# Decoder layer on one core: denominator sums by two merged DMA chains, projection in f16 parts

## The reference

```python
q = heads(x @ Wq)                      # x is layer-normed; 16 heads of 32
k_s, v_s = x @ Wkv_short;  k_l, v_l = x @ Wkv_long
bias = -abs(pos[None, :] - pos[:, None]) * (1 - decay_factor)
out = alpha * attention(q, k_s, v_s, bias) + (1 - alpha) * attention(q, k_l, v_l, None)
x = x + out @ Wo
x = x + cross_attention(ctx, layernorm(x), mask)
x = x + fp4_linear(silu(gate(x)) * up(x), w_down)    # gate, up: fp4_linear too
```

## Time and profile before

| | before |
|---|---|
| median of 3 runs | 5346.45 us |
| profiled execution | 5346.38 us |
| its span | 5344.6 us |
| busy over the span: PE, DVE, ACT, POOL | 96%, 77%, 54%, 50% |
| mean granted TensorE clock | 0.986 |
| moved by DMAs that POOL issues (q0) | 469.79 MB |

### The profile page before, as it was taken

The page is one execution under the profiler, slowest core; times in us unless marked ns, Lnnn a source line. Parts: engine busy times, 40 slices in busy tenths (PEclk is TensorE's granted clock), DMA queues, the critical chain, the costliest instruction groups (busy, mean ns, idle before and its releaser), DMA issues. The chain is left out here.

```text
span 5344.6 us, 96126 instructions
## 1 busy us (share of the span) xinstructions
PE 5140.3 (96%) x27244; PEld 2119.3 (40%) x27244; DVE 4123.0 (77%) x7218; ACT 2889.4 (54%) x5201; POOL 2657.0 (50%) x978
## 2 busy tenths in 40 slices
PE   7999899999999999999999999999977999999999
PEld 3444333333333333333333333333324555555555
DVE  5345588888888888888888888888845777777776
ACT  1112157776767777767677777777753333333332
POOL 0000067888878878788787877878870000000000
PEclk9999889999999999999999999999998999999999
DMA  4323356766777677677777767767651000000000
GB/s 138 105 92 105 102 123 168 178 165 170 171 173 172 167 176 167 169 174 171 173 166 174 171 167 176 168 169 174 158 136 53 24 18 18 24 18 18 24 18 12
DMA packets 210066, 660.43 MB, mean 124 GB/s; under 512 B 25668, under 2 KB 105156, under 8 KB 152198
## 3 DMA queue, kind: packets, MB, share of 16 engines
q0 software_dynamic: 64512, 469.79, 37.8%
q1 hardware_dynamic: 145159, 185.65, 11.5%
HBM read 123.56 MB, written 61.64 MB: 35 GB/s over the span
## 5 line engine op out<-in xcount | busy, mean ns | idle before, releaser
L791 DVE TENSOR_REDUCE rowmax_parts<-scores_qk 128x1 f32<-128x512 f32 x4096 | 2525.6, 679 | 467.4 <-PE scores_qk L863 467.4
L772 ACT ACTIVATE probs_T<-scores_kq 128x512 f32<-128x512 f32 x4096 | 2286.6, 597 | 984.2 <-PE scores_kq L863 919.9
L707 POOL TENSOR_TENSOR probs_added<-probs_added,probs_T 128x2048 f32<-128x2048 f32 x448 | 2030.1, 4532 | 461.0 <-ACT probs_T L772 449.6
L863 PE MATMUL scores_kq<-q_operand,k_operand 103*128 103x512 f16 (+3 forms) x3712 | 1274.6, 349 | 10.6 <-ACT probs_T L772 8.7
L863 PE MATMUL scores_qk<-k_operand,q_operand 96*128 96x512 f16 (+4 forms) x3712 | 1121.9, 351 | 44.0 <-DMA k_operand<-positions_dram 18.9
L934 PE MATMUL outputs_T<-probs_T,v_operand 128*32 128x512 f32 x8192 | 1091.9, 605 | 4.9 <-ACT probs_T L772 4.9
L863 PEld LDWEIGHTS scores_kq<-q_operand,k_operand 103*128 103x128 f16 x3712 | 358.3, 97 | 921.3 <-ACT probs_T L772 636.0
L1381 PE MATMUL f_gate_up<-w_gate_up,xq_T 128*128 128x352 f32 x2048 | 627.2, 462 | 0.8 <-issue 0.8
L863 PEld LDWEIGHTS scores_qk<-k_operand,q_operand 96*128 96x128 f16 (+1 forms) x3712 | 354.7, 98 | 438.8 <-DVE rowmax_parts L791 185.5
L1381 PEld LDWEIGHTS f_gate_up<-w_gate_up,xq_T 128*128 128x128 f32 x2048 | 382.5, 190 | 202.5 <-issue 2.9
L707 POOL TENSOR_TENSOR probs_added<-probs_T 128x2048 f32<-128x2048 f32 x64 | 290.3, 4536 | 242.4 <-ACT probs_T L772 242.4
(11 more groups left out here) (148 smaller groups left out, 3834.9 us busy)
## 6 DMA issues: line engine op xcount, KB each, us to landing
probs_poured<-probs_T POOLq DMA_DIRECT2D x448, 1024.0 KB, 7.3
qk_parts_dram<-qk_parts SPq DMA_DIRECT2D x96, 256.0 KB, 2.5
q_operand<-qk_parts_dram SPq DMA_DIRECT2D x192, 128.0 KB, 2.6
k_operand<-qk_parts_dram SPq DMA_DIRECT2D x192, 128.0 KB, 3.1
v_dram<-v_heads SPq DMA_DIRECT2D x16, 1024.0 KB, 5.6
v_operand<-v_dram SPq DMA_DIRECT2D x64, 256.0 KB, 6.3
q_operand_above<-qk_parts_dram SPq DMA_DIRECT2D x96, 128.0 KB, 2.8
x_groups<-x SPq DMA_DIRECT2D x8, 1024.0 KB, 8.8
```

The costliest lines, as they stand in the source:

```text
L707: nc.gpsimd.tensor_tensor(total, first, probs[:, b % PBUF, :], ALU.add).then_inc(added.sem, 1)
L772: nc.scalar.activation(probs[:, kb % PBUF, qt * BANK:(qt + 1) * BANK], pb[:, k % 2, :], ACT.Exp)\
L791: nc.vector.reduce_max(rowmax[:, w % 2, c // NQ, c % NQ:c % NQ + 1], pa[:, k % 3, :], AX.X)\
L863: return nc.tensor.matmul(out, lhsT, rhs, start=start, stop=stop, skip_group_check=True)
```

## The change

1. **Denominator.** GpSimd adds the ten blocks 0, 1, 2, 3, 4, 7, 10, 13, 14, 15 (9 adds a unit, before 8). ScalarE writes the exps of blocks 6 and 5 straight into `probs_poured0` and `probs_poured1`, which are out of the ring of 8. On these bases the two chains add blocks 9 and 12, and blocks 8 and 11. After the add of block 13 GpSimd waits for both chains and issues one more adding DMA, `merge`, from `probs_poured1` to `probs_poured0`. TensorE counts two sums instead of three, both in the next unit, at blocks 2 and 3.
2. **Loops.** The 14 middle passes become 2 turns of 7 passes; on GpSimd, whose loop has all 16 passes, 8 turns of 2.
3. **Projection.** The turned x and the weights (times 64) are split into two f16 parts each, and a product is three f16 matmuls, hi x hi, hi x lo and lo x hi, for each f32 matmul before. ScalarE and GpSimd split the weights once, ScalarE and VectorE each turned x. The scale is taken back where the products leave PSUM.
4. **Quantiser.** The scratch tile `t` is gone; its steps are done in the destination.

```diff
-BY_POOL = (0, 1, 3, 5, 7, 9, 11, 13, 14)
-BY_DMA = ((2, 6, 10), (4, 8, 12, 15))
+BY_POOL = (0, 1, 2, 3, 4, 7, 10, 13, 14, 15)
+BASE = (6, 5)
+BY_DMA = ((9, 12), (8, 11))
+MERGE_AFTER = 13
-COUNT_POURED = (14, KB + 3)
-COUNT_ADDED = KB + 1
+POURS = (3, 2)
+COUNT_POURED = KB + 2
+COUNT_ADDED = KB + 3
+def probs_of(w, kb):
+    return poured_sum[BASE.index(kb)][:, :] if kb in BASE else probs[:, ring_place(w, kb), :]
 def pour(w, n, b, c):
     i = BY_DMA[c].index(b)
     wait_apart(pool, expd, expd.at(n, (w * KB + b + 1) * NQ), passed)
     if i == 0:
-        wait_apart(pool, counted_poured[c], counted_poured[c].at(n, w), passed)
-        nc.gpsimd.dma_start(poured_sum[c][:, :], probs[:, b % PBUF, :]).then_inc(poured[c].sem, 16)
+        wait_apart(pool, summed, summed.at(n, w * KB + BASE[c] + 1), passed)
     else:
         wait_apart(pool, poured[c], poured[c].at(n, w * POURS[c] + i), passed)
-        nc.gpsimd.dma_start(poured_sum[c][:, :], probs[:, b % PBUF, :], accum_op=ALU.add)\
-            .then_inc(poured[c].sem, 16)
+    nc.gpsimd.dma_start(poured_sum[c][:, :], probs_of(w, b), accum_op=ALU.add).then_inc(poured[c].sem, 16)
+def merge(w, n):
+    wait_apart(pool, poured[0], poured[0].at(n, (w + 1) * POURS[0] - 1), passed)
+    wait_apart(pool, poured[1], poured[1].at(n, (w + 1) * POURS[1]), passed)
+    nc.gpsimd.dma_start(poured_sum[0][:, :], poured_sum[1][:, :], accum_op=ALU.add).then_inc(poured[0].sem, 16)
 # ScalarE, before the exps of block kb
+    if kb == BASE[0]:
+        act.wait_ge(counted_poured.sem, counted_poured.at(n, w))
+    elif kb == BASE[1]:
+        if w or not first:
+            act.wait_ge(poured[0].sem, poured[0].at(n, w * POURS[0]))
 # TensorE
+def counts(w, n, i):
+    if i == COUNT_POURED:
+        pe.wait_ge(sums_out.sem, sums_out.at(n, w))
+        pe.wait_ge(poured[0].sem, poured[0].at(n, (w + 1) * POURS[0]))
+        count(poured_sum[0], counted_poured, True, False)
     if i == COUNT_ADDED:
+        pe.wait_ge(added.sem, added.at(n, (w + 1) * ADDS))
+        count(added_sum[:, w % 2, :], counted, False, True)
 # loops of the attention
-with nc.Fori(1, PASSES - 1, engines=[pe.engine], hint_back_edge=True) as n:
-    one_pass(n, False, False)
+with nc.Fori(0, (PASSES - 2) // TURN, engines=[pe.engine], hint_back_edge=True) as m:
+    for i in range(TURN):
+        one_pass(m * TURN + (i + 1), False, False)
 # projection
+PRODUCTS = ((0, 0), (0, 1), (1, 0))
 for c in range(KT):
-    last = nc.tensor.matmul(mm[:, m % 4, :], w[:, c, m * P:(m + 1) * P], xT[:, u, c, :],
-                            start=c == 0, stop=c == KT - 1)
+    for a, b in PRODUCTS:
+        last = nc.tensor.matmul(mm[:, m % 4, :], w_parts[:, a, c, m * P:(m + 1) * P], xT[:, u, c, b, :],
+                                start=c == 0 and a == b, stop=c == KT - 1 and a == 1)
+def split_turned(n, u):                      # VectorE
+    for c in range(KT):
+        dve.wait_ge(copied.sem, copied.at(n, c + 1))
+        nc.vector.tensor_tensor(xT[:, u, c, 1, :], tp[:, c % 2, :], xT[:, u, c, 0, :], ALU.subtract)
```

More of the change, by code:

```diff
@@ L355, in _ @@
             nc.gpsimd.memset(eps[:, :], EPS).then_inc(consts, 1)
+            for i in range(5):
+                own = slice(i * H, (i + 1) * H)
+                pool.wait_ge(w_hi, i + 1)
+                nc.gpsimd.tensor_scalar(w[:, :, own], w[:, :, own], UPSCALE, None, ALU.mult).then_inc(w_scaled, 1)
+                pool.wait_ge(w_scaled, i + 1)
+                nc.gpsimd.tensor_tensor(w_parts[:, 1, :, own], w[:, :, own], w_parts[:, 0, :, own], ALU.subtract)\
+                    .then_inc(w_lo, 1)
         @block.vector
@@ L508 @@
 PBUF = 8
+TURN = 7
 PARTS3 = 3 * HD
@@ L518, with ring_place @@
 MIX = 11
-BY_POOL = (0, 1, 3, 5, 7, 9, 11, 13, 14)
-BY_DMA = ((2, 6, 10), (4, 8, 12, 15))
+BY_POOL = (0, 1, 2, 3, 4, 7, 10, 13, 14, 15)
+BASE = (6, 5)
+BY_DMA = ((9, 12), (8, 11))
+MERGE_AFTER = 13
 ADDS = len(BY_POOL) - 1
-POURS = [len(blocks) for blocks in BY_DMA]
-COUNT_POURED = (14, KB + 3)
-COUNT_ADDED = KB + 1
+POURS = (3, 2)
+IN_RING = [b for b in range(KB) if b not in BASE]
+RING = len(IN_RING)
+COUNT_POURED = KB + 2
+COUNT_ADDED = KB + 3
 TAKE_SUMS = 5
+def ring_place(w, kb):
+    return (w * RING + IN_RING.index(kb)) % PBUF
 def adds_until(kb):
@@ L678, in _ @@
             one_pass(0, True, False)
-            with nc.Fori(1, PASSES - 1, engines=[sp.engine], hint_back_edge=True) as n:
-                one_pass(n, False, False)
+            with nc.Fori(0, (PASSES - 2) // TURN, engines=[sp.engine], hint_back_edge=True) as m:
+                for i in range(TURN):
+                    one_pass(m * TURN + (i + 1), False, False)
             one_pass(PASSES - 1, False, True)
@@ L706, in add @@
                     wait_apart(pool, added, added.at(n, w * ADDS + adds_until(b) - 1), passed)
-                nc.gpsimd.tensor_tensor(total, first, probs[:, b % PBUF, :], ALU.add).then_inc(added.sem, 1)
+                nc.gpsimd.tensor_tensor(total, first, probs_of(w, b), ALU.add).then_inc(added.sem, 1)
             def pour(w, n, b, c):
@@ L725, in one_pass @@
                             add(w, n, b)
-                        else:
-                            pour(w, n, b, int(b in BY_DMA[1]))
-            with nc.Fori(0, PASSES, engines=[pool.engine], hint_back_edge=True) as n:
-                one_pass(n)
+                        for c in range(2):
+                            if b in BY_DMA[c]:
+                                pour(w, n, b, c)
+                        if b == MERGE_AFTER:
+                            merge(w, n)
+            with nc.Fori(0, PASSES // 2, engines=[pool.engine], hint_back_edge=True) as m:
+                for i in range(2):
+                    one_pass(m * 2 + i)
         @block.scalar
@@ L847, in _ @@
             one_pass(0, True, False)
-            with nc.Fori(1, PASSES - 1, engines=[dve.engine], hint_back_edge=True) as n:
-                one_pass(n, False, False)
+            with nc.Fori(0, (PASSES - 2) // TURN, engines=[dve.engine], hint_back_edge=True) as m:
+                for i in range(TURN):
+                    one_pass(m * TURN + (i + 1), False, False)
             one_pass(PASSES - 1, False, True)
```

106 lines of the change are left out of this document (59 added, 47 removed).

## The result

The changed kernel takes 5715.14 us (median of 4 runs, 5711.98 to 5718.41), the kernel before 5346.38 us (4 runs): a ratio of 1.069, with a 95% interval of 1.0672 to 1.0709. The forecast was 5810 us, 1.087 times, with a range of 5390 to 5970. Direction and place were right. The size was 95 us too high, and a second stall that no step of the forecast mentions sits in every unit.

What follows compares the result with a forecast made beforehand. It took TensorE, with the exps that it waits for, to set the unit's time before the change. The profiled 5346.4 us, +543 for the attention and -77 for the projection gave 5812, say 5810 us, range 5390 to 5970.

Steps and rivals of the forecast that it cites:

- The served transfers: Attention, block 8's issue to the merge's: four DMAs run one behind the other, 23.6 us; this case has 0.77.
- landings of 11 us and more: Sign in the attention that the case is right: issues at blocks 9 and 12 land after 11 us and more.
- The share without a gap: Sign in the attention that the case is right: DMA share without a gap over four transfers.
- Both rivals with overlap: Paired transfers in the attention: full overlap, about 5230 us, 0.13 (with no cost); partial overlap, about 5400 us, 0.10.
- POOL's period: POOL's row per attention unit: 57.4 to 61.2 us, taken as 60.0, more than TensorE's 50.6.
- the loads: Next pass's loads in the attention: 3.8 us of engine time, two thirds falling before the merge.
- The wait at block 2: TensorE idle about 8 us a unit before L1009 in block 2, where the count waits for the merge.
- The removed count: One count fewer per attention unit on TensorE: 0.89 us each, 57 us over 64; unit becomes 50.6 us.
- The projection: Start and projection with f16 products: -90 + 7 + 5.5 = -77 us, bounds -92 to -65.
- VectorE's chain: Projection start: ScalarE splits the other four blocks before its first copy, delaying this chain by 3.8 us.
- the weights' split on POOL: Projection start: POOL's one-input instruction isn't in the trace; the sum stays within 1 us either way.
- Loops at 0: Loops: fewer back edges save TensorE only a little, and it no longer sets the pace: 0.

Runs made afterwards that it cites:

- weigh_at_12: The changed kernel with VectorE's weigh and the mix behind it at block 12 instead of 10: 5762.46 us (1.0782).
- half_and_weigh_12: The changed kernel with half the columns in each adding DMA and the merge, and weigh and mix at block 12: 5353.67 us (1.0015).
- spread_weigh_at_10: The changed kernel with DMAs at blocks 7, 9, 11, 12, merge after 14, poured sum's count one block later, weigh and mix at 10, 11: 5523.17 us.
- spread: The changed kernel with DMAs at blocks 7, 9, 11, 12, merge after 14, poured sum's count one block later, weigh and mix at 12: 5246.15 us.
- projection_low_by_dve: The kernel before with the f16 projection and smaller quantiser scratch, VectorE instead of POOL making the weights' low parts: 5300.76 us (0.9924).

## Why the prediction was right, and where its sizes were off

The balance: the attention, from its first start to the last count, was forecast at +543 us. Measured, from 640.66 to the count at 4367.93, it is 3727.3 us, +428.5 against the earlier trace rows. The start and projection were forecast at -77 and came to 640.66 - 697.78 = -57.1. The sum is 5346.4 + 428.5 - 57.1 = 5717.8, and the profiled execution took 5717.4. So the forecast was 114 us too high in the attention and 20 too low in the projection, and the second error hid part of the first.

- **The served transfers: right.** 24.7 us in the mean from block 8's issue to the merge's, for 23.6 without loads and 26.2 with those that I put in. Of the landings of 11 us and more that I named, block 9's came (median 11.8); block 12's has a median of 10.4, and 7.9 us in the unit read above, where it was issued late behind the stalled exps. The share without a gap, another sign, came only in weigh_at_12 (0.98 for 0.91). Half the bytes and a better spacing each took the limit away, so serving one behind the other was the cause, as the forecast had it. Both rivals with overlap fall: their stretches were 17.3 and 18.4 to 20 us. The Trainium skill, *DMA: Bandwidth & Descriptors*, "SWDGE vs HWDGE vs iDMA", with its single queue for what GpSimd issues, agrees with these rows.
- **POOL's period: right in kind, 60.0 for 58.2.** The step that was mis-sized is the loads: I put two thirds of 3.8 us before the merge, 2.6, and their packets take 1.6 us there. The stretch came to 24.7 for 26.2, the rest of POOL's row to 33.5 for 33.8. Over 63 periods the 1.8 us are 113, nearly the whole of the error in the attention.
- **The wait at block 2: right in sum, wrong in place.** I had all of it, about 8 us, before L1009. By the starts of L1002, block 2 is 3.1 us longer in the changed kernel than without a wait, and blocks 10 and 11 together 5.4 us longer than in half_and_weigh_12. That stall is missing in the forecast, and only 111.5 us in all stay at L1009. In weigh_at_12, without the stall, block 2 is 9.1 us longer and the wait comes to 400.2. The total was right only because the two overlap, and that was luck.
- **The missed step: the weigh.** The forecast moved POOL's adds and never asked which instruction of VectorE runs beside each of them. Had the transfers been well placed, this alone would have made the kernel slower: spread_weigh_at_10 is at 5523. GpSimd's order of before, shown with the change, has a DMA at block 10 where the change has an add. In the unit read before, the weigh began at 2018.43, 0.10 us behind the end of the add of block 9. A reader of VectorE's row of before would have found the weigh at 742 ns and its worst case at 4310 ns. The Trainium skill states it, *SBUF — State Buffer*, "SBUF: two separate sides": VectorE in a two-port mode, or with two SBUF inputs against a GpSimd instruction that reads SBUF, and GpSimd take a shared pair of ports as an exclusive lock, held for the whole instruction. Here 742 ns became 3.6 to 3.9 us, ending 0.55 us after POOL's add, and the kernel before, changed by one digit, shows the same. The trace agrees, and the rule should have been weighed.
- **The removed count: right.** By the starts of L1002 the units of half_and_weigh_12 without a mix took 50.04 us (median), where those of before with the same inputs took 51.06: a count is worth the 0.89 or a little more. spread has a mean of 50.87 for 51.46, with the weigh and the mix together at block 12 of every second unit.
- **The projection: later groups right, the first wrong.** The five groups behind the first took 59.6 to 62.2 us for 59.7 and 60.6, the two of six jobs 70.33 and 63.0 for 71.5 and 62. The first product came 5.0 us later than before, for 1.7, and the first group took 86.5 us, for 64.4 (60.6 and the 3.8 of VectorE's chain). The mis-sized term is the weights' split on POOL, priced "within 1 us". projection_low_by_dve takes 3.3 us off the start and 19.5 us off the first group, where the quantiser's instructions had waited for POOL's. I had looked at how long POOL would take, not at whom it would keep out.
- **Loops at 0: right for TensorE behind POOL, wrong as a statement on the edit.** Beside the f16 projection they save 44 us. The first half is argued: no run takes the loops out of the changed kernel.

## What to carry to other kernels

When work moves onto GpSimd, or along its row, list for every one of its instructions which VectorE instruction runs beside it; those with two SBUF inputs, and fast one-input ones, wait until it ends, and one that stands on the critical path costs its wait and TensorE's clock after it. Transfers that each fill the DMA engines want as much other work between their issues as one of them lasts: with the weigh at block 12, as many adds and transfers took 59.0 us a unit bunched and 50.9 spread. Two limits in one stage hide each other, so an experiment that removes one and gains nothing doesn't show that it costs nothing; remove both, singly and together.

## What was not expected of the hardware

- A VectorE instruction of 0.74 us takes 3.6 us beside a GpSimd add of 4.5 us, one of 0.43 us takes 4.16 us beside a GpSimd subtraction of 4.1 us. Reductions from PSUM (677 ns, and 679 before), the reciprocals (0.94 us before and after) and instructions with one input in PSUM kept their times beside the same adds (L404: 684 ns in the slow first group, 685 over all).
- A wait of 2.9 us on VectorE costs 4.4 us a unit: the granted clock of TensorE in the stretches read behind it is 0.50, 0.50 and 0.62.
- An adding transfer of 1 MB lands after 6.9 us at the least, one of 512 KB after 4.5; 2.1 us behind another, the large one landed after 12.4.
- A back edge of the loop of passes cost TensorE about 3 us with one version of the code ahead of it, and next to nothing with another.
